# Mixture kernel on one core: convolution rotations as one 1024-column VectorE operation, and a later hand-over of the carry

## The chip, the cores and the metric

The kernel runs on one core of one Trainium2 chip. The metric is the device time of one execution in microseconds (us). Beside the plain runs there is one profiled execution; its trace carries all durations used here.

## The reference

The reference is two layers of the form `x = x + s * silu(g)`, on a normalised `x` of 2048 tokens by 512 channels. In the first layer `s` is a gated product with a per-token top-k mask, and `g` a product with ternary weights. In the second layer `g` is a 512x512 product (with low-rank experts folded in), and `s` is a small recurrent network, which the change touches. It has 2 sequences of 1024 steps, 64 channels and 4 blocks. Cut to what matters:

```python
def sconv(x, phazor_c, last_conv_c):          # x: (2, 1024, 64), per block
    p = jnp.tanh(r) * jnp.exp(1j * jnp.angle(phazor_c))
    # conv[t] = sum_{s<=t} p**(t-s) * x[s]  +  last_conv * p**(t+1), computed by FFT
    return conv.real

def body(h, p):                               # four times
    y = silu(layernorm(h, l1w, l1b))
    h = h + sconv(y, pr + 1j * pi, lr + 1j * li) * scl
    y = layernorm(h, l2w, l2b)
    y = silu(y @ w1.T + b1_) @ w2.T + b2_
    return h + y
```

## The kernel before, in words

The first 469 us of the trace are the first layer and the folding of weights; the change does not touch them. Then comes the recurrent part. Channels lie on partitions (64 for each of the two sequences, 128 in all), time steps on columns, and the 1024 steps are cut into two halves of 512 columns, `c` = 0 and 1.

The convolution is a complex recurrence with a constant factor `p = rho * e^(i*angle)`. The kernel turns the input backwards by the angle, so that the recurrence has the real factor `rho`, runs two real scans, and turns the result back. In steps, for block `l` and half `c`:

- `turn` (L1547): VectorE computes `w_re = y * rot_c`. GpSimd computes `w_im = y * rot_s` (`times_sin`, L1352).
- `scan` (L1558), twice on VectorE: `u_re` from `w_re`, then `u_im` from `w_im`. For half 0 the start value is `u0`; for half 1 it is `carry`.
- `turn_back` (L1563): VectorE computes `w_re = u_re * rot_c`, and GpSimd `w_im = u_im * rot_s` (`times_sin` again, L1352).
- `hand_over` (L1571 to L1576), half 0 only: four operations of one column on VectorE. They make `carry` from the last column of `u_re` and `u_im`, for half 1 in the next phase.
- `into_h`: VectorE adds `w_re + w_im` (L1582) and adds the scaled sum to the residual stream `h` (L1584). The latter raises `h_ready`.

The work runs in ten phases. Phase p mixes (layer norm and convolution) half `p % 2` of block `p // 2`, and feeds (layer norm and the two products of the feed-forward part) the half that phase p - 1 mixed. Order within an engine is the program's order. What matters around the change:

- TensorE (PE) begins a phase with `center_rows` (L1737), which needs the `h` that the last phase's `into_h` wrote. Then come a gate product (L1763, the 512x512 product of the second layer's `g`, cut into pieces that fill in), the variances (L1744), the spreading of the factors (L1752), the up products (L1776) and the down products (L1782). It ends with the down products. Ahead of phase 1 it does `project_in(1)` (L1730).
- VectorE: at a phase's start `variance` (`lnv`, L1529) for both halves, `widen` (L1534) and `normed` (L1542) for both, then the convolution, and last `fed` (L1589), which adds the down products to `h`. In phase 0 there is no `fed`; `h_in(1)` (L1525) and `take_means` (L1615) stand at its end. `h_in(1)` moves the projected input of half 1 from PSUM into `h`, and ACT's `squares` (L1433) of phase 1 waits for it.
- GpSimd (POOL) makes the tables `rot_c` and `rot_s` of the coming blocks, three steps of 512 columns a phase (L1335). Two steps stand at the start of a phase, behind a wait for the `h_ready` of the last `fed` (in phase 1: of phase 0's `into_h`). The two `root` operations (`lnr`, L1346) stand behind them, each of which needs `lnv`. A third table step follows behind `ln_w`, and then the two `times_sin`. From phase 7 on no table step is left, and in phase 6 one at the start.

`settled` only raises a semaphore. Every data product between engines, and between operations of one engine, goes through a counted semaphore.

Of the kernel before, what the change touches and what calls it, by code (L numbers as in the profile page):

```python
# [13 lines left out]
P = 128  # L14
# [28 lines left out]
NB = 512  # L43
# [20 lines left out]
def settled(engine, passed):  # L64


    engine.sem_inc(passed, 1)


def mixture_kernel(nc, x, wg_t, wu_t, wd_t, tern_w, ffn_bias, win_t, cols, last_cols, b1_cols,  # L70
# [7 lines left out]
    with ExitStack() as ctx:  # L78
# [43 lines left out]
        work = over_weights(4 * SEQ)  # L122
        xn = work.rearrange("p (t n) -> p t n", n=HID)
        w_re, w_im, u_re, u_im = (work[:, j * SEQ:(j + 1) * SEQ] for j in range(4))
        sq = w_re
        weff = over_weights(KH, HID)
        win = over_weights(KH, DIM)
# [150 lines left out]
        with ExitStack() as actx:  # L278
            def sb(name, shape, dt=F32):
                return actx.enter_context(nc.sbuf_tensor(name, shape, dt))  # L280
# [867 lines left out]
        with ExitStack() as bctx:  # L1148
# [20 lines left out]
            xc = sb("xc", [P, SEQ])  # L1169
            lnv = sb("lnv", [P, HALVES, 8])  # L1170
            lnr = sb("lnr", [P, HALVES, 8])
            rot_c = sb("rot_c", [P, DEPTH, NB])
            rot_s = sb("rot_s", [P, DEPTH, NB])
            tbig = sb("tbig", [P, NB])
            rho = sb("rho", [P, DEPTH])
            part = sb("part", [P, 2])
# [5 lines left out]
            def by_half(name):  # L1182
                return [sem(f"{name}{c}") for c in range(HALVES)]
# [32 lines left out]
            ln_bc = by_half("ln_bc")  # L1216
            ln_y = by_half("ln_y")
            ln_o = by_half("ln_o")
            cv_wr = by_half("cv_wr")
            cv_wi = by_half("cv_wi")  # L1220
            cv_ur = by_half("cv_ur")
            cv_ui = by_half("cv_ui")
            cv_a = by_half("cv_a")
            cv_b = by_half("cv_b")
            cv_ab = by_half("cv_ab")
            cy_t = sem("cy_t")
            cy = sem("cy")
# [25 lines left out]
            def cs(c):  # L1253
                return slice(c * NB, (c + 1) * NB)
# [55 lines left out]
            def _(pool):  # L1310
# [34 lines left out]
                    pool.wait_ge(ln_v[c], q + 1)  # L1345
                    pool.tensor_tensor(lnr[:, c, :], lnv[:, c, :], expo2[:], ALU.pow).then_inc(ln_r[c], 1)  # L1346

                def times_sin(l, c, src, ready, count, done):

                    pool.wait_ge(ready[c], count)  # L1350
                    settled(pool, pool_passed)
                    pool.tensor_tensor(w_im[:, cs(c)], src[:, cs(c)], rot_s[:, l, :], ALU.mult).then_inc(done[c], 1)  # L1352

                def residual(m):
                    if on_pool(m):
                        t = ORDERED[m]
# [26 lines left out]
                root(0, 0)  # L1383
                pool.wait_ge(ln_w[0], 1)
                tables_some(6, 8)
                times_sin(0, 0, y, ln_o, 1, cv_wi)
                times_sin(0, 0, u_im, cv_ui, 1, cv_b)
                for phase in range(1, PHASES):
                    l, c = mixing(phase)
                    k, d = feeding(phase)  # L1390
                    feeds = phase < PHASES - 1
                    if l < DEPTH:
                        if phase == 1:
                            pool.wait_ge(h_ready[0], 2)
                        else:
                            pool.wait_ge(h_ready[c], 2 * l + 1)
                        tables_some(5 + 3 * phase, 7 + 3 * phase)
                    root(2 * l, c)
                    if feeds:
                        root(2 * k + 1, d)  # L1400
                    if l < DEPTH:
                        pool.wait_ge(ln_w[d], 2 * k + 2)
                        tables_some(7 + 3 * phase, 8 + 3 * phase)
                    if l < DEPTH:
                        pool.wait_ge(tb, N_SMALL + 6 * l + 6)
                        times_sin(l, c, y, ln_o, 2 * l + 1, cv_wi)
                        times_sin(l, c, u_im, cv_ui, l + 1, cv_b)
                    elif feeds:
                        for m in range(4):
                            residual(m)  # L1410
                    else:
                        for m in range(4, TILES):
                            residual(m)

# [84 lines left out]
            def _(dve):  # L1499
# [42 lines left out]
                    dve.tensor_tensor(xc[:, cs(c)], h[:, cs(c)], bank2[c], ALU.mult).then_inc(ln_y[c], 1)  # L1542

                def turn(l, c):
                    dve.wait_ge(tb, N_SMALL + 6 * l + 6)
                    dve.wait_ge(ln_o[c], 2 * l + 1)
                    dve.tensor_tensor(w_re[:, cs(c)], y[:, cs(c)], rot_c[:, l, :], ALU.mult).then_inc(cv_wr[c], 1)  # L1547

                def scan(l, c, imaginary):
                    w, u, ready, done = (w_im, u_im, cv_wi, cv_ui) if imaginary else (w_re, u_re, cv_wr, cv_ur)  # L1550
                    dve.wait_ge(ready[c], l + 1)
                    j = int(imaginary)
                    if c == 0:
                        first = u0[:, j, l:l + 1]
                    else:
                        dve.wait_ge(cy, 2 * l + 2)
                        first = carry[:, j:j + 1]
                    dve.tensor_tensor_scan(u[:, cs(c)], rho[:, l:l + 1].to_broadcast([P, NB]), w[:, cs(c)],  # L1558
                                           first, ALU.mult, ALU.add).then_inc(done[c], 1)

                def turn_back(l, c):
                    dve.wait_ge(cv_ur[c], l + 1)
                    dve.tensor_tensor(w_re[:, cs(c)], u_re[:, cs(c)], rot_c[:, l, :], ALU.mult).then_inc(cv_a[c], 1)  # L1563

                def hand_over(l):

# [11 lines left out]

                def into_h(l, c):
                    dve.wait_ge(cv_a[c], l + 1)  # L1580
                    dve.wait_ge(cv_b[c], l + 1)
                    dve.tensor_tensor(w_re[:, cs(c)], w_re[:, cs(c)], w_im[:, cs(c)], ALU.add).then_inc(cv_ab[c], 1)  # L1582
                    dve.wait_ge(cv_ab[c], l + 1)
                    dve.scalar_tensor_tensor(out=h[:, cs(c)], in0=w_re[:, cs(c)], scalar=pcol(l, C_SCL),  # L1584
                                             in1=h[:, cs(c)], op0=ALU.mult, op1=ALU.add).then_inc(h_ready[c], 1)

                def fed(l, c):
                    dve.wait_ge(ff_2[c], l + 1)
                    dve.scalar_tensor_tensor(out=h[:, cs(c)], in0=bank1[c], scalar=bias_c[:, l:l + 1],  # L1589
                                             in1=h[:, cs(c)], op0=ALU.add, op1=ALU.add).then_inc(h_ready[c], 1)  # L1590
# [61 lines left out]
                for phase in range(PHASES):  # L1652
# [20 lines left out]
                    if l < DEPTH:  # L1673
                        turn(l, c)
                        scan(l, c, False)
                        scan(l, c, True)
                        turn_back(l, c)
                        if c == 0:
                            hand_over(l)
                        into_h(l, c)  # L1680
                        if feeds:
                            fed(k, d)
                    elif feeds:
                        output(0)
                        output(1)
                        residual(1)
                        output(2)
                        output(3)
                        fed(k, d)
                    else:  # L1690
                        residual(5)
                        residual(7)
                        for m in range(PER_HALF, TILES):
                            output(m)
                            if m > PER_HALF:
                                residual(m - 1)
                        residual(TILES - 1)
# [223 lines left out]
```

## Time and profile before

| | us |
|---|---|
| median of 3 runs | 656.93 |
| the three runs | 655.63, 656.93, 657.48 |
| the profiled execution | 658.63 |
| its span | 656.8 |
| busy in the span: PE | 614.6 |
| DVE (VectorE) | 483.6 |
| ACT | 327.6 |
| POOL (GpSimd) | 169.6 |

The span is what the rows of the trace cover; 1.83 us of the profiled execution lie outside it. A row of the timeline has the start in us, the duration in us, the engine, the line of the kernel and the operation with what it writes and reads; in brackets stands how long the engine sat idle before it and what released it. When neighbouring rows of one engine are merged, `x2` stands at the end.

### The profile page before, as it was taken

The numbers are of one execution on the slowest core, as the hardware profiler recorded it, in microseconds if no ns is written. First come the engines' busy times: TensorE is split into PE (matmuls) and PEld (weight loads), VectorE is DVE, ScalarE is ACT, GpSimd is POOL, SyncE is SP. The second block draws the span as 40 slices with busy tenths as digits, with TensorE's granted clock in tenths as the row PEclk, the third lists the DMA queues.
The fourth block names the chain that finished last, engine by engine and source line by source line (L and its number), as shares of the span: only waits on it lengthen the run. The fifth ranks groups of instructions, "written<-read, shape, count | busy, mean of one in ns | idle before, by whom it ended". The sixth has DMA issues, their size and how long they took to land. (4 is left out here: it accounts for less than half of the span.)

```text
span 656.8 us, 8597 instructions
## 1 busy us (share of the span) xinstructions
PE 614.6 (94%) x2772; PEld 448.0 (68%) x2772; DVE 483.6 (74%) x938; ACT 327.6 (50%) x547; POOL 169.6 (26%) x296
## 2 busy tenths in 40 slices
PE   4798889999999999999999999989889999999985
PEld 3687778888888888888888888846754444444432
DVE  6798887888797787778778777767777555556556
ACT  5669467447528428627725744832273333334330
POOL 1000001001001000200200100598485555543334
PEclk9988999999999999999999999989889999999997
DMA  8811000200300200110020010640020000000015
GB/s 299 316 45 65 0 1 0 97 1 0 96 0 0 96 0 0 64 32 0 0 96 0 0 65 1 227 135 1 4 63 1 0 1 0 1 0 1 0 64 193
DMA packets 17181, 32.32 MB, mean 49 GB/s; under 512 B 3224, under 2 KB 3736, under 8 KB 17152
## 3 DMA queue, kind: packets, MB, share of 16 engines
q1 hardware_dynamic: 17152, 31.97, 14.2%
q8 instruction: 14, 0.23, 0.2%
q14 instruction: 15, 0.12, 0.1%
HBM read 24.62 MB, written 7.34 MB: 49 GB/s over the span
## 5 line engine op out<-in xcount | busy, mean ns | idle before, releaser
L751 DVE TENSOR_SCALAR_CACHE_REDUCE junk_d<-k_buf,cand 128x1376 int8<-128x1376 f32 x56 | 91.9, 1640 | 0.3
L582 ACT ACTIVATE junk_a<-k_buf,cand 128x1376 int8<-128x1376 f32 x56 | 80.5, 1437 | 0.6
L563 ACT ACTIVATE s_buf<-ps_a 128x1376 f32<-128x1376 f32 x16 | 21.1, 1320 | 105.4 <-PE ps_a L988 92.6
L1015 PE MATMUL ps_a<-wd_hi,zt_hi 128*128 128x512 f32 (+1 forms) x176 | 71.8, 408 | 1.9 <-DVE zt_lo L864 1.0
L1015 PE MATMUL ps_a<-wd_hi,zt_lo 128*128 128x512 f32 (+1 forms) x176 | 69.2, 393 | 0.0
L1015 PE MATMUL ps_a<-wd_lo,zt_hi 128*128 128x512 f32 (+1 forms) x176 | 69.0, 392 | 0.0
L1763 PE MATMUL ps_b<-arena,xt 128*128 128x512 f32 x128 | 65.4, 623 | 0.0
L504 POOL TENSOR_TENSOR xres<-xres,gate 128x512 f32<-128x512 f32 x12 | 23.6, 1965 | 144.5 <-DVE gate L871 144.5
L496 POOL TENSOR_TENSOR rstd<-var_eps,expo 128x2 f32<-128x2 f32 x8 | 5.6, 705 | 204.3 <-DVE var_eps L692 204.3
L988 PE MATMUL ps_a<-wg_hi,xt_hi 128*128 128x512 f32 (+1 forms) x192 | 53.2, 386 | 1.1 <-DVE xt_lo L680 1.1
L988 PE MATMUL ps_b<-wu_hi,xt_hi 128*128 128x512 f32 (+1 forms) x192 | 51.7, 377 | 1.5 <-DVE s_buf L729 1.5
L988 PE MATMUL ps_a<-wg_hi,xt_lo 128*128 128x512 f32 (+1 forms) x192 | 51.7, 378 | 0.0
L988 PE MATMUL ps_a<-wg_lo,xt_hi 128*128 128x512 f32 (+1 forms) x192 | 51.4, 377 | 0.0
L988 PE MATMUL ps_b<-wu_hi,xt_lo 128*128 128x512 f32 (+1 forms) x192 | 50.5, 371 | 0.0
L988 PE MATMUL ps_b<-wu_lo,xt_hi 128*128 128x512 f32 (+1 forms) x192 | 49.8, 367 | 0.0
L864 DVE TENSOR_TENSOR zt_lo<-ps_t,zt_hi 128x512 fp32r<-128x512 f32 (+1 forms) x48 | 30.8, 641 | 25.3 <-ACT zt_hi L619 24.5
L1440 ACT ACTIVATE y<-xc,arena 128x512 f32<-128x512 f32 x18 | 14.7, 815 | 53.1 <-DVE xc L1542 53.1
L988 PEld LDWEIGHTS ps_a<-wg_hi,xt_hi 128*128 128x128 f32 x192 | 35.2, 195 | 7.0 <-DVE xt_lo L680 1.5
L619 ACT ACTIVATE zt_hi<-ps_t 128x512 fp32r<-128x512 f32 (+1 forms) x48 | 26.9, 563 | 25.9 <-PE ps_t L1001 21.9
L988 PEld LDWEIGHTS ps_a<-wg_lo,xt_hi 128*128 128x128 f32 x192 | 35.7, 194 | 5.8
L1015 PEld LDWEIGHTS ps_a<-wd_hi,zt_hi 128*128 128x128 f32 (+1 forms) x176 | 33.1, 188 | 9.1 <-DVE zt_lo L864 1.8
L988 PEld LDWEIGHTS ps_a<-wg_hi,xt_lo 128*128 128x128 f32 x192 | 35.3, 193 | 5.9
(229 smaller groups left out, 1285.6 us busy)
## 6 DMA issues: line engine op xcount, KB each, us to landing
xin<-in_x SPq DMA_DIRECT2D x8, 512.0 KB, 3.6
xres<-in_x SPq DMA_DIRECT2D x8, 512.0 KB, 3.4
out<-arena SPq DMA_DIRECT2D x16, 256.0 KB, 2.0
x_scratch<-xres SPq DMA_DIRECT2D x6, 512.0 KB, 3.0
arena<-x_scratch SPq DMA_DIRECT2D x3, 1024.0 KB, 11.8
m_buf<-in_wd_t SPq DMA_DIRECT2D x3, 512.0 KB, 9.8
m_buf<-in_wg_t SPq DMA_DIRECT2D x2, 688.0 KB, 5.4
k_buf<-in_wg_t SPq DMA_DIRECT2D x2, 688.0 KB, 7.9
```

The lines of the kernel that those rows point to most:

```text
L496: pool.tensor_tensor(rstd[:], var_eps[:], expo[:], ALU.pow).then_inc(ln_rs, 1)
L504: pool.tensor_tensor(row, xres[:, t, :], gate2[:, t, :], ALU.add).then_inc(x1_ready, 1)
L563: act.activation(s_buf[:, t, :], ps_a[:].rearrange("p a n -> p (a n)")[:, 0:INNER], ACT.Silu).then_inc(s_ready, 1)
L582: act.activation(junk_a[:], k_buf[:, 1, :], ACT.Sign, bias=c, scale=-1.0, accum_out=below[:, 1:2]).then_inc(act_step, 1)
L619: act.activation(zt_hi[:, c0 * P:c1 * P], ps_t[:, i % 2, 0:(c1 - c0) * P], ACT.Copy).then_inc(zt_h, 1)
L751: dve.tensor_scalar(junk_d[:], k_buf[:, 0, :], c, -float(DROP), ALU.is_lt, ALU.add, accum_out=e).then_inc(cnt_dve, 1)
L864: dve.tensor_tensor(zt_lo[:, c0 * P:c1 * P], ps_t[:, i % 2, 0:(c1 - c0) * P], zt_hi[:, c0 * P:c1 * P].bitcast(F32), ALU.subtract).then_inc ...
L988: last = pe.matmul(bank[:, c, 0:c1 - c0], xs, ws[:, k, c0:c1], start=(k == 0 and n == 0), stop=(k == KH - 1 and n == 2))
L1015: last = pe.matmul(ps_a[:, t, :], zs, ws[0:rows, c, :], start=(c == 0 and n == 0), stop=(c == CHUNKS - 1 and n == 2))
L1440: act.activation(y[:, cs(c)], xc[:, cs(c)], func, scale=w, bias=b).then_inc(ln_o[c], 1)
L1763: pe.matmul(bankg[k % 2], xt[:, n, t * P:(t + 1) * P], weff[:, n, :], start=(n == 0), stop=False)
```

## The change

GpSimd's 16 `times_sin` (two for each block and half) are gone. The two tables become one tensor `rot` with the cosine and the sine of a block side by side, and `w_re`/`w_im` and `u_re`/`u_im` are also addressed in pairs (`w_both`, `u_both`). `turn` is one VectorE operation of 2x512 columns, with `y` read twice; it raises `cv_w`, for which both scans wait. `turn_back` is one VectorE operation of 2x512 columns and waits for both scans. `hand_over` moves from between `turn_back` and `into_h` to behind `into_h` and, where there is one, behind `fed`.

```diff
+        w_both, u_both = (work[:, 2 * j * SEQ:2 * (j + 1) * SEQ].rearrange("p (j n) -> p j n", j=2) for j in range(2))
...
-            rot_c = sb("rot_c", [P, DEPTH, NB])
-            rot_s = sb("rot_s", [P, DEPTH, NB])
+            rot = sb("rot", [P, DEPTH, 2, NB])
+            rot_c, rot_s = rot[:, :, 0, :], rot[:, :, 1, :]
...
-                def times_sin(l, c, src, ready, count, done):
-
-                    pool.wait_ge(ready[c], count)
-                    settled(pool, pool_passed)
-                    pool.tensor_tensor(w_im[:, cs(c)], src[:, cs(c)], rot_s[:, l, :], ALU.mult).then_inc(done[c], 1)
...
-                times_sin(0, 0, y, ln_o, 1, cv_wi)
-                times_sin(0, 0, u_im, cv_ui, 1, cv_b)
...
-                    if l < DEPTH:
-                        pool.wait_ge(tb, N_SMALL + 6 * l + 6)
-                        times_sin(l, c, y, ln_o, 2 * l + 1, cv_wi)
-                        times_sin(l, c, u_im, cv_ui, l + 1, cv_b)
-                    elif feeds:
+                    if l == DEPTH and feeds:
...
                 def turn(l, c):
+
                     dve.wait_ge(tb, N_SMALL + 6 * l + 6)
                     dve.wait_ge(ln_o[c], 2 * l + 1)
-                    dve.tensor_tensor(w_re[:, cs(c)], y[:, cs(c)], rot_c[:, l, :], ALU.mult).then_inc(cv_wr[c], 1)
+                    dve.tensor_tensor(w_both[:, :, cs(c)],
+                                      y[:, cs(c)].rearrange("p (o n) -> p o n", o=1).to_broadcast([P, 2, NB]),
+                                      rot[:, l, :, :], ALU.mult).then_inc(cv_w[c], 1)
...
                 def turn_back(l, c):
                     dve.wait_ge(cv_ur[c], l + 1)
-                    dve.tensor_tensor(w_re[:, cs(c)], u_re[:, cs(c)], rot_c[:, l, :], ALU.mult).then_inc(cv_a[c], 1)
+                    dve.wait_ge(cv_ui[c], l + 1)
+                    dve.tensor_tensor(w_both[:, :, cs(c)], u_both[:, :, cs(c)], rot[:, l, :, :],
+                                      ALU.mult).then_inc(cv_a[c], 1)
...
                 def into_h(l, c):
                     dve.wait_ge(cv_a[c], l + 1)
-                    dve.wait_ge(cv_b[c], l + 1)
...
                         turn_back(l, c)
-                        if c == 0:
-                            hand_over(l)
                         into_h(l, c)
                         if feeds:
                             fed(k, d)
+                        if c == 0:
+                            hand_over(l)
```

## Rows read from the trace of the kernel before

**Rows 1.** Busy time by engine in one phase, PE first; then clock, DMA.

```profile
530.90:548.30 17.40, 16.94 (x62) 7.36 (x61) 9.32 (x13) 6.75 (x11) 9.35 (x7) 1.00 0.01 1
```

**Rows 2.** The chain that ended last, start of phase 3: start us, us, what.

```profile
531.04 0.76 DVE arena L1589
531.99 1.28 POOL rot_c L1335
533.44 1.06 POOL tbig L1335
534.50 1.60 POOL lnr L1346
```

**Rows 3.** Timeline, start of phase 3: VectorE's first variance.

```profile
533.74 0.17 DVE L1529 TENSOR_SCALAR lnv<-ps_b 128x8 f32<-128x8 f32 x1 [1.95 <-PE ps_b L1744]
```

**Rows 4.** Timeline, phase 3 (half 1): the convolution, and what needs it.

```profile
539.69 1.69 DVE L1547 TENSOR_TENSOR arena<-y,rot_c 128x512 f32<-128x512 f32 x1
...
541.42 2.46 DVE L1558 TENSOR_TENSOR_SCAN arena<-rho,carry,arena 128x512 f32<-128x512 f32 x2
...
545.57 2.76 PE L1782 MATMUL ps_a<-arena,w 128*64 128x512 f32 x8
...
546.06 0.69 DVE L1582 TENSOR_TENSOR arena<-arena 128x512 f32<-128x512 f32 x1 [1.60 <-POOL arena L1352]
...
546.79 0.75 DVE L1584 SCALAR_TENSOR_TENSOR arena<-arena 128x512 f32<-128x512 f32 x1
...
548.26 1.13 PE L1737 MATMUL ps_a<-arena,center 128*128 128x512 f32 x2
```

**Rows 5.** Timeline, phase 2 (half 0): turning back, hand-over, sum, next phase's first product.

```profile
526.46 0.67 DVE L1563 TENSOR_TENSOR arena<-arena,rot_c 128x512 f32<-128x512 f32 x1
526.72 1.53 POOL L1352 TENSOR_TENSOR arena<-arena,rot_s 128x512 f32<-128x512 f32 x1 [3.22 <-DVE arena L1558]
...
527.41 0.86 DVE L1574 SCALAR_TENSOR_TENSOR carry<-arena,part 128x1 f32<-128x1 f32 x1
...
528.19 0.21 DVE L1576 SCALAR_TENSOR_TENSOR carry<-arena,part 128x1 f32<-128x1 f32 x1
...
528.24 2.76 PE L1782 MATMUL ps_a<-arena,w 128*64 128x512 f32 x8
...
529.08 0.75 DVE L1584 SCALAR_TENSOR_TENSOR arena<-arena 128x512 f32<-128x512 f32 x1
...
530.93 1.13 PE L1737 MATMUL ps_a<-arena,center 128*128 128x512 f32 x2
```

**Rows 6.** Groups by line with shapes apart: VectorE's 1024-column product of two SBUF tensors.

```profile
L675 DVE TENSOR_TENSOR wd_lo<-m_buf,wd_hi 128x1024 fp32r<-128x1024 f32 x3 | 3.6, 1219 | 0.0
```

**Rows 7.** Timeline, phase 0 from its convolution on, and the start of phase 1.

```profile
489.25 0.69 DVE L1547 TENSOR_TENSOR arena<-y,rot_c 128x512 f32<-128x512 f32 x1
...
492.98 3.65 PE L1730 MATMUL ps_a<-xt,arena 128*64 128x512 f32 x16
...
495.87 0.75 DVE L1584 SCALAR_TENSOR_TENSOR arena<-arena 128x512 f32<-128x512 f32 x1
...
496.69 0.75 DVE L1525 TENSOR_SCALAR arena<-ps_a,bias_c 128x512 f32<-128x512 f32 x1
496.83 1.27 POOL L1335 TENSOR_TENSOR rot_c<-rot_c,tbig 128x512 f32<-128x512 f32 x1 [1.79 <-DVE arena L1584]
...
497.35 1.29 DVE L1615 TENSOR_TENSOR w<-w,off 128x512 f32<-128x512 f32 x1
497.47 0.63 ACT L1433 ACTIVATE arena<-arena 128x512 f32<-128x512 f32 x1 [3.79 <-DVE arena L1525]
...
498.28 1.29 POOL L1335 TENSOR_TENSOR tbig<-arena 128x512 f32<-128x512 f32 x1 [0.18 <-POOL rot_c L1335]
...
498.50 0.95 PE L1744 MATMUL ps_b<-means,arena 128*128 128x2 f32 x8
...
499.74 3.24 POOL L1346 TENSOR_TENSOR lnr<-lnv,expo 128x8 f32<-128x8 f32 x2 [0.16 <-DVE lnv L1529]
```

More of the change, by code:

```diff
@@ L1218, in mixture_kernel @@
             ln_o = by_half("ln_o")
-            cv_wr = by_half("cv_wr")
-            cv_wi = by_half("cv_wi")
+            cv_w = by_half("cv_w")
             cv_ur = by_half("cv_ur")
@@ L1223, in mixture_kernel @@
             cv_a = by_half("cv_a")
-            cv_b = by_half("cv_b")
             cv_ab = by_half("cv_ab")
@@ L1403, in _ @@
                         tables_some(7 + 3 * phase, 8 + 3 * phase)
-                    if l < DEPTH:
-                        pool.wait_ge(tb, N_SMALL + 6 * l + 6)
-                        times_sin(l, c, y, ln_o, 2 * l + 1, cv_wi)
-                        times_sin(l, c, u_im, cv_ui, l + 1, cv_b)
-                    elif feeds:
+                    if l == DEPTH and feeds:
                         for m in range(4):
                             residual(m)
-                    else:
+                    elif l == DEPTH:
                         for m in range(4, TILES):
@@ L1546, in turn @@
                     dve.wait_ge(ln_o[c], 2 * l + 1)
-                    dve.tensor_tensor(w_re[:, cs(c)], y[:, cs(c)], rot_c[:, l, :], ALU.mult).then_inc(cv_wr[c], 1)
+                    dve.tensor_tensor(w_both[:, :, cs(c)],
+                                      y[:, cs(c)].rearrange("p (o n) -> p o n", o=1).to_broadcast([P, 2, NB]),
+                                      rot[:, l, :, :], ALU.mult).then_inc(cv_w[c], 1)
                 def scan(l, c, imaginary):
-                    w, u, ready, done = (w_im, u_im, cv_wi, cv_ui) if imaginary else (w_re, u_re, cv_wr, cv_ur)
-                    dve.wait_ge(ready[c], l + 1)
+                    w, u, done = (w_im, u_im, cv_ui) if imaginary else (w_re, u_re, cv_ur)
+                    dve.wait_ge(cv_w[c], l + 1)
                     j = int(imaginary)
```

## The prediction

> **What bounds the kernel now.** I read the table of busy time by stretch first. In phase 3, taken from one `center_rows` to the next, PE is busy for 16.94 of 17.40 us, VectorE for 9.32 and GpSimd for 9.35 [rows 1]. So the recurrent part goes at PE's pace, and the two engines that the change works on have slack over a phase. The next question is whether either of them ends a wait of PE somewhere.
>
> The chain that ended last answers for the start of a phase [rows 2]. `fed` ends at 531.04 + 0.76 = 531.80. Then the chain goes through GpSimd: the table step `rot_c` at 531.99, the table step `tbig` at 533.44, and the root at 534.50. VectorE's `lnv`, for which the root waits too, was done at 533.74 + 0.17 = 533.91 [rows 3]. So the table steps, not `lnv`, let the root go in that phase, and about half a microsecond is lost there. The change keeps these table steps and their wait; it takes `times_sin` away, which stands at the end of a phase.
>
> The timeline answers for the end of a phase. In phase 3 `into_h` ends at 546.79 + 0.75 = 547.54, and the `center_rows` that needs it starts at 548.26: 0.72 us of slack [rows 4]. In phase 2 `into_h` ends at 529.08 + 0.75 = 529.83 and `center_rows` starts at 530.93: 1.10 us of slack [rows 5]. In both cases PE is in its down products until then; in phase 2 that row ends at 528.24 + 2.76 = 531.00 [rows 5]. `fed` waits for the same down products, not for the convolution. The two starts of `center_rows` are 17.33 us apart, and nothing of the convolution is in that distance.
>
> **The change part by part.**
>
> *Turning.* The product in phase 3 shows 1.69 us for 512 columns, against 0.67 for the same size in `turn_back` [rows 4, 5]; the difference is the GpSimd product beside it. A VectorE product of two 1024-column tensors in SBUF took 1.219 us where GpSimd did nothing [rows 6]. That row has another output type and no repeated operand; two separate 512-column products would be 2 x 0.67 = 1.34, which I take as the upper end. I take 1.22 for `turn` and 1.22 for `turn_back`.
>
> *Both scans.* They stay: 2.46 us for the pair [rows 4]. No GpSimd product stands beside them any more. `turn_back` now waits for the second scan too; I count 0.04 for each hand-over between dependent operations, as between 546.06 + 0.69 = 546.75 and 546.79 [rows 4].
>
> *Sum for the convolution.* From the start of `turn` to the end of `into_h`: 1.22 + 2.46 + 1.22 + 0.69 + 0.75 + 4 x 0.04 = 6.50 us. In phase 3 it was 547.54 - 539.69 = 7.85 [rows 4], so `into_h` ends 1.35 us sooner. In phase 2 the two last operations start behind the hand-over; `turn` had the same place in the phase, one period before 539.69, at 522.36, which makes 529.83 - 522.36 = 7.47 and a gain of 0.97. All of this is gained ahead of a PE that is busy with down products for another 0.72 and 1.10 us anyway. **It is worth nothing on the path**: PE reaches `center_rows` at the same time, only with more slack. The cover would have to shrink by over 2 us before this gain counted. On the other side, if both products took twice 1.22, `into_h` would end at about 547.54 - 1.35 + 2.44 = 548.63 in phase 3, 0.4 late in each phase; no row points there.
>
> *GpSimd without `times_sin`.* Sixteen products go. Behind them in GpSimd's queue stand the next phase's table steps, which wait for `fed` (released at 531.80, started at 531.99 [rows 2]), long after the old product's end at 526.72 + 1.53 = 528.25 [rows 5]. They start when they did. Worth nothing.
>
> *The moved hand-over, phases 2, 4 and 6.* Its four operations now start when `fed` ends, in the time in which VectorE waited 1.95 us for PE's variances [rows 3]. What is queued behind them is `lnv`, and for `lnv` waits the root. The trace shows what a GpSimd operation does to them. In phase 2 the first two (one tensor each) went through beside GpSimd's product, but the third, L1574, which reads two tensors in SBUF, took 0.86 us and ended at 528.27, just as GpSimd's product did at 528.25 [rows 5]. L1576 followed within 528.19 to 528.40 [rows 5]. Now GpSimd's `rot_c` starts 0.19 behind `fed`. L1574 started 527.41 - 527.13 = 0.28 behind the end of the operation ahead of the hand-over [rows 5]. So GpSimd should be first by about 0.09, L1574 ends with it at 531.99 + 1.28 = 533.27, and L1576 at about 533.4. `lnv` is due at 533.74 [rows 3]. Cost nothing, with 0.3 us in hand. Behind phase 6 GpSimd has no table step, so nothing is blocked.
>
> *The moved hand-over, phase 0.* Here there is no `fed`; `h_in(1)` stands behind it, and PE's input product ends at 492.98 + 3.65 = 496.63 [rows 7]. New end of `into_h`: 489.25 + 6.50 = 495.75, instead of 496.62 [rows 7]. `center_rows` still waits for PE's own product until 496.63, so nothing is gained. GpSimd's `rot_c` starts 0.21 behind `into_h` (496.83 against 496.62 [rows 7]), now at 495.96, and ends at 497.23. The third operation of the hand-over comes at 496.03 and is blocked until then; the fourth ends at about 497.35. So `h_in(1)` starts at about 497.35 instead of 496.69, 0.66 late. ACT's square of that half was done at 497.47 + 0.63 = 498.10 and PE's variances started at 498.50 [rows 7]: 0.40 of it is covered, less the 0.05 between ACT's end and PE. **Cost: 0.66 - 0.35 = 0.3 us**, once, since the root of phase 1 started at 499.74 directly behind `lnv` [rows 7]; the table steps will be done at about 498.5 and don't hold it.
>
> The sum is 658.63 + 0.3 = 658.9 for a profiled execution. This execution lies 1.70 us over the median of 656.93. I put the same 0.3 on the median: **657.2 us**.
>
> *A rule of the skill against the trace.* L1571 and L1572, of one column, took their 0.2 us while GpSimd's product ran, since L1574 behind them had already started at 527.41 within it [rows 5]. The Trainium skill, "SBUF — State Buffer", section "Who interferes with whom", says that `tensor_scalar` can enter a two-port mode and then contends with GpSimd, and that the first one holds the pair for its whole instruction. By the trace these two don't; if they did, the hand-over would only come a gap later, which is the second rival below.
>
> **The rivals.**
>
> *1. VectorE is first.* 0.09 us between L1574 and GpSimd's step is little. If L1574 gets in ahead, the hand-over is over at about 496.3 in phase 0, `h_in(1)` waits for PE as before, and the cost is 0; in phases 3 and 5 the first table step may start up to 0.1 later, and the root with it. Result 656.9 to 657.1. It can't be told from the forecast by the time, but by the start of `h_in(1)`.
>
> *2. The hand-over misses the gap: slower.* Between two table steps GpSimd pauses for 0.18 us [rows 7]. If L1576 doesn't get in there, it is blocked a second time until `tbig` ends. Phase 0: `tbig` would run from 497.41 for 1.06 [rows 2] to 498.47, `h_in(1)` would start at 498.55, that is 1.86 late, and the variances 1.86 - 0.35 = 1.5 late. Phases 3 and 5: `tbig` ends at 534.50, `lnv` at 534.8, and the root 0.25 behind the start of `lnv` instead of with `tbig`, at 534.9 instead of 534.50: 0.4 each. Together 2.3 us, and 659.2. Against it: L1615 began at 497.35 beside GpSimd's step (to 498.10), ended at 498.64, so it did the rest of its work directly behind 498.10, and the next step, started at 498.28, took 1.29 instead of 1.06 [rows 2, 7]. A waiting VectorE operation gets in, and GpSimd waits. But it was one operation, and here a second one must follow it; L1576 did so within 0.15 us of the release, but with no GpSimd step behind [rows 5]. It decides from the point at which L1576 starts later than 0.18 us behind GpSimd's end.
>
> *3. The convolution was on the path after all: faster.* PE's rows have modelled ends. If the down products truly ended sooner and `center_rows` waited for `into_h`, each of the eight phases could gain up to what `into_h` gains, but no more than to the next bound. Against it: phases 2 and 3 have a slack of 1.10 and 0.72 and still the same distance from the start of the down products to `center_rows`, 530.93 - 528.24 = 2.69 [rows 5] and 548.26 - 545.57 = 2.69 [rows 4]; a wait for `into_h` would make them differ. If a third of the 1.35 counted in seven phases, it would be -3.2 us: 653.8.
>
> The page "Perfetto Trace Analysis" of the Trainium skill (section "Identifying the Most-Contended Engine") says to optimise the engine with the highest occupancy first. By that rule a change that leaves PE's work alone brings nothing here; the rows above say the same for a reason of place, not of share.
>
> **How the numbers follow.** The forecast (+0.3) gets 0.50, the first rival 0.25, the second 0.12, the third 0.08, and 0.05 is for what I don't see. A measurement of this kernel can tell about 0.3% from no change, 2 us. The forecast and the first rival are within it. The second rival at +2.3 is at its edge: two thirds of it count as slower. With the unseen split evenly: faster 0.10, same 0.79, slower 0.11. The runs of before alone spread from 655.63 to 657.48, so a median can move by 1 us without a cause; the forecast with that is 656.0 to 658.3. For 8 in 10 I go from 655.5 to 659.0, which takes in most of the second rival and a small gain.
>
> **What would show it.** In the trace of after: `turn` and `turn_back` at 1.22 us each; `into_h` ending about 2 us ahead of `center_rows` in every phase, which still starts 2.7 us behind the first down product; periods of 17.3 us unchanged; L1574 at some 1.2 us behind `fed` in phases 2 and 4, and short in phase 6; `h_in(1)` 0.7 us later in phase 0, and the roots of phases 3 and 5 still behind `tbig`. The prediction is wrong if the period of the phases changes by more than 0.1 us either way, if `lnv` in phases 3 and 5 starts more than 1.95 us behind `fed`, or if a 1024-column product takes much over 1.34.

## The result, and the profile after

| | median of 13 runs, us | lowest to highest |
|---|---|---|
| before | 657.02 | 655.26 to 658.23 |
| changed | 659.28 | 657.84 to 661.35 |

The ratio is 1.0039, with a 95% interval of 1.0024 to 1.0053. The changed kernel is slower by 2.3 us by the medians (1.6 to 3.5 by the interval). A second set of 11 runs of it, beside 29 of the kernel before, gave 1.0044 (1.0030 to 1.0058). The median lies above the forecast's range, which was 657.2 within 655.5 to 659.0.

The page of the changed kernel shows PE where it was, 0.6 us more, and GpSimd with 22.4 us less:

```profile
span 657.3 us, 8564 instructions
...
PE 615.2 (94%) x2772; PEld 447.9 (68%) x2772; DVE 485.7 (74%) x938; ACT 327.3 (50%) x547; POOL 147.2 (22%) x280
```

The spans of the two profiled executions (656.8 and 657.3) can't be subtracted. The first layer, which the change does not touch, ended 2.14 us earlier in the second one: its first transposition of the recurrent part starts at 467.62, against 469.76. So I compared the traces piece by piece, from one `center_rows` to the next.

The phases from the second on are as forecast. This is phase 3 of the changed kernel, by the timeline (start us, us, engine, line, operation):

```profile
539.72 1.22 DVE L1535 TENSOR_TENSOR arena<-y,rot 128x1024 f32<-128x1024 f32 x1
...
540.98 2.46 DVE L1548 TENSOR_TENSOR_SCAN arena<-rho,carry,arena 128x512 f32<-128x512 f32 x2
...
543.54 1.23 DVE L1554 TENSOR_TENSOR arena<-arena,rot 128x1024 f32<-128x1024 f32 x1
...
544.80 0.69 DVE L1573 TENSOR_TENSOR arena<-arena 128x512 f32<-128x512 f32 x1
...
545.53 0.75 DVE L1575 SCALAR_TENSOR_TENSOR arena<-arena 128x512 f32<-128x512 f32 x1
...
545.61 2.76 PE L1773 MATMUL ps_a<-arena,w 128*64 128x512 f32 x8
...
548.29 1.13 PE L1728 MATMUL ps_a<-arena,center 128*128 128x512 f32 x2
```

They stand to [rows 4]. The products take 1.22 and 1.23 us, the convolution 546.28 - 539.72 = 6.56 us (6.50 was worked out), and `center_rows` still starts 2.68 behind the first down product, now with 2.0 us of slack. The hand-over behind phase 2 goes as worked out too:

```profile
532.03 1.26 POOL L1334 TENSOR_TENSOR rot<-rot,tbig 128x512 f32<-128x512 f32 x1 [9.72 <-DVE arena L1580]
532.11 1.21 DVE L1566 SCALAR_TENSOR_TENSOR carry<-arena,part 128x1 f32<-128x1 f32 x1
...
533.24 0.21 DVE L1568 SCALAR_TENSOR_TENSOR carry<-arena,part 128x1 f32<-128x1 f32 x1
533.48 1.06 POOL L1334 TENSOR_TENSOR tbig<-arena 128x512 f32<-128x512 f32 x1 [0.18 <-POOL rot L1334]
...
533.78 0.17 DVE L1516 TENSOR_SCALAR lnv<-ps_b 128x8 f32<-128x8 f32 x1 [0.33 <-PE ps_b L1735]
```

The third operation is blocked by GpSimd for its whole table step, the fourth gets into the gap, and `lnv` still waits for PE, for 0.33 us. It stands to [rows 2, 3] as it should.

Phase 1 is the place where most of the loss lies. From its first `center_rows` to the next it took 16.91 us before and 19.20 us (494.43 to 513.63) in the changed kernel. Its start, by the timeline, answers to [rows 7]:

```profile
493.00 0.75 DVE L1575 SCALAR_TENSOR_TENSOR arena<-arena 128x512 f32<-128x512 f32 x1
...
493.96 1.27 POOL L1334 TENSOR_TENSOR rot<-rot,tbig 128x512 f32<-128x512 f32 x1 [6.81 <-DVE arena L1575]
494.03 1.21 DVE L1566 SCALAR_TENSOR_TENSOR carry<-arena,part 128x1 f32<-128x1 f32 x1
...
494.43 1.13 PE L1728 MATMUL ps_a<-arena,center 128*128 128x512 f32 x2
...
495.16 0.21 DVE L1568 SCALAR_TENSOR_TENSOR carry<-arena,part 128x1 f32<-128x1 f32 x1
495.29 0.73 DVE L1512 TENSOR_SCALAR arena<-ps_a,bias_c 128x512 f32<-128x512 f32 x1
...
495.40 1.06 POOL L1334 TENSOR_TENSOR tbig<-arena 128x512 f32<-128x512 f32 x1 [0.18 <-POOL rot L1334]
...
496.75 1.05 PE L1735 MATMUL ps_b<-means,arena 128*128 128x2 f32 x8 [0.33 <-ACT arena L1420]
...
498.55 3.56 PE L1754 MATMUL ps_b<-arena,xt 128*128 128x512 f32 x4
```

Two things are to be seen. First, the forecast blocking: the hand-over's third operation ends with GpSimd's table step, `h_in(1)` (L1512) starts 0.86 us behind the first `center_rows`, PE runs dry for 0.33 us, and the variances start 496.75 - 494.43 = 2.32 us behind `center_rows`. Before it was 1.82. Second, something that no part of the forecast had: the gate products behind the variances take 3.56 us instead of 1.96. The busy time by stretch shows why. The columns are PE, PEld, DVE, ACT and POOL busy, then the granted clock:

```profile
494.40:498.50 4.10, 3.77 (x22) 2.43 (x20) 2.78 (x5) 1.60 (x3) 2.31 (x3) 1.00 0.02 4
498.50:502.00 3.50, 3.50 (x7) 1.33 (x7) 0.59 (x2) 0.00 (x0) 2.82 (x2) 0.54 0.00 0
```

For 3.5 us PE had a clock of 0.54, so nearly all of it at 1.2 GHz, right behind the stretch with the gap. It costs 1.6 us in the gate products and some 0.2 in the transpositions behind them.

### The profile page after: what moved, and what is told of

Same layout as the page of the kernel before. It is cut to its first block and busy times, and to the rows that moved or that the text cites. A ratio compares the mean times of both kernels' runs of the same rounds, so it can differ in the third digit from the quotient of the medians.

```text
span 657.3 us, 8564 instructions
## 1 busy us (share of the span) xinstructions
PE 615.2 (94%) x2772; PEld 447.9 (68%) x2772; DVE 485.7 (74%) x938; ACT 327.3 (50%) x547; POOL 147.2 (22%) x280
## 5 line engine op out<-in xcount | busy, mean ns | idle before, releaser
L1754 PE MATMUL ps_b<-arena,xt 128*128 128x512 f32 x128 | 67.4, 640 | 0.0
```

The source lines that it names most:

```text
L1754: pe.matmul(bankg[k % 2], xt[:, n, t * P:(t + 1) * P], weff[:, n, :], start=(n == 0), stop=False)
```

## The experiments

Two questions come first: is it the rotations or the hand-over, and is it phase 0's hand-over or the later ones? Theory 1 (T1 in the expectations) says that the late `h_in(1)` is the whole cause, through a direct delay and the low clock.

**1. The rotations alone.** On the changed kernel:

```diff
                         turn_back(l, c)
+                        if c == 0:
+                            hand_over(l)
                         into_h(l, c)
                         if feeds:
                             fed(k, d)
-                        if c == 0:
-                            hand_over(l)
```

> The changed kernel with the hand-over back in its old place ahead of the sum into h; so only the rotations are changed. Theory (T1): the whole cost lies in phase 1 and comes from the hand-over, which delays h_in(1) by some 0.85 us, lets PE run dry for 0.33 us and is followed by a stretch of PE at 1.2 GHz. Then this kernel costs nothing: 657.0 (between 656.5 and 657.5), phase 1 from its first center product to its row product 7.63 us as before, no low clock there. Rival (T2): the 1024-column rotations themselves change what PE sees (y, rot and w read and written in another rhythm). Then the cost stays: 659.3, with the low clock in phase 1.

Measured: 657.54 (12 runs) beside 657.71, ratio 1.0001 (0.9984 to 1.0018). Phase 1 took 16.91 us, at full clock. With GpSimd idle the hand-over's third operation takes 0.22 us:

```profile
494.76 0.22 DVE L1566 SCALAR_TENSOR_TENSOR carry<-arena,part 128x1 f32<-128x1 f32 x1
494.89 0.21 DVE L1568 SCALAR_TENSOR_TENSOR carry<-arena,part 128x1 f32<-128x1 f32 x1
```

The rotations alone cost nothing that these runs can tell; the interval leaves room for about 1 us either way.

**2. The hand-over alone.** On the kernel before, the same edit the other way round.

> The kernel before with nothing but the hand-over moved behind the sum into h and behind the feed-forward sum. T1: the sum into h ends at about the time of PE's center product in phase 0 (it still waits for GpSimd), the hand-over starts only then and is blocked by GpSimd's table step for 1.3 us, so h_in(1) comes over 1.5 us late. PE waits over 1 us, and the clock falls as in the changed kernel or longer: 657.0 + 1.2 + 1.7 = 660. T2 (the rotations are the cause): 657.3 at most, from the uncovered part of the delay, at full clock.

Measured: 659.88 (7 runs) beside 657.71, ratio 1.0047 (1.0030 to 1.0063). `h_in(1)` came 1.48 us behind `center_rows`, PE waited 0.95 us for it, and phase 1 took 18.13 us. The clock stayed full there in this trace, against the expectation. `center_rows` itself came 10.32 us behind the spreading product of phase 0, against 9.86 in the trace of before; experiment 5 comes back to that. The time is close to the expected 660, but in this trace by other parts: 1.22 us in phase 1, 0.3 to 0.5 ahead of it, and 0.42 in the last two phases.

**3. Only phase 0's hand-over moved on.** On the changed kernel:

```diff
-                        if c == 0:
+                        if c == 0 and phase:
                             hand_over(l)
...
                         h_in(1)
                         take_means(w2[:], KH, 2 * DEPTH, w2_s)
+                        hand_over(0)
```

> The changed kernel with the hand-over of phase 0 alone put behind h_in(1) and the subtraction of the means of w2; phases 2, 4 and 6 as changed. T1: h_in(1) on time, the cost is gone: 657.0 (656.5 to 657.5), and the hand-overs of phases 2, 4, 6 cost nothing. Rival (T3): part of the cost comes from the three later hand-overs, blocked behind fed; then 657.5 or more stays, and a later phase shows a period over 17.33 us.

Measured: 657.18 (12 runs) beside 657.71, ratio 1.0002 (0.9988 to 1.0017). Phases 1 to 7 took 16.91, 17.33, 17.32, 17.34, 17.32, 16.92 and 16.94 us, as in the kernel before. The hand-overs of phases 2, 4 and 6 cost nothing, and the whole loss sits in phase 0's.

**4. Four traces of the changed kernel.** Does the low clock come every time? These are the trace above and three more.

> The changed kernel once more, for a second trace of it. T1: the stretch of PE at 1.2 GHz in phase 1 comes again at the same place (the first gate products behind the variances of phase 1), since the delay that leads to it is fixed by the program; +2.3 us. Rival (T4): the low clock there was chance of one execution (the two traces also differ by some 2 us in the first layer); then this trace has none and the difference to before is about 0.5 us, or the runs fall in two groups.

> A third trace of the changed kernel, to see how often the low clock in phase 1 comes. So far phase 1 took 19.20 us with it in one trace and 17.97 without in the other. If it is a matter of where the earlier low stretch in phase 0 falls, the third trace shows one of these two lengths, and h_in(1) between 0.8 and 1.4 behind the first center product.

> A fourth trace of the changed kernel, for the same question. If the direct cost were all, phase 1 would be 17.4 to 18.0 in each; the mean of the runs (+2.1 us in all, 0.3 of it outside the span) asks for about 18.7 on average, so one of these two should show over 19.

Worked out from the starts of the rows of the four traces, in us:

| trace | `h_in(1)` behind `center_rows` | PE's gap ahead of the variances | variances behind `center_rows` | low clock | phase 1 |
|---|---|---|---|---|---|
| first | 0.86 | 0.33 | 2.32 | yes | 19.20 |
| second | 1.33 | 0.80 | 2.78 | no | 17.97 |
| third | 1.33 | 0.80 | 2.78 | no | 17.97 |
| fourth | 0.91 | 0.38 | 2.36 | yes | 19.26 |
| before, both traces | 0.01, -0.14 | none | 1.82 | no | 16.91 |

So it comes in two forms. With the small gap, the gap is followed by some 3.5 us of low clock. This is the fourth trace; the gate row, the last one, had taken 1.96 us in the kernel before:

```profile
496.60 1.05 PE L1735 MATMUL ps_b<-means,arena 128*128 128x2 f32 x8 [0.38 <-ACT arena L1420]
497.52 1.03 PE L1735 MATMUL ps_a<-means,arena 128*128 128x2 f32 x8
498.41 3.63 PE L1754 MATMUL ps_b<-arena,xt 128*128 128x512 f32 x4
```

and in the second trace, with the larger gap, it isn't:

```profile
497.00 1.05 PE L1735 MATMUL ps_b<-means,arena 128*128 128x2 f32 x8 [0.80 <-ACT arena L1420]
497.91 1.03 PE L1735 MATMUL ps_a<-means,arena 128*128 128x2 f32 x8
498.81 1.96 PE L1754 MATMUL ps_b<-arena,xt 128*128 128x512 f32 x4
```

The direct cost is 17.97 - 16.91 = 1.06 us in one form. In the other it is 0.5 and the clock takes another 1.8. The mean of the four is 1.7 us. Which form comes is seen half a phase earlier, at the spreading product of phase 0, where PE always has a low stretch. In the second trace it covers that product; VectorE waits longer for it, and its convolution ends later against PE:

```profile
484.56 1.11 PE L1743 MATMUL ps_a<-ident,arena 128*128 128x128 f32 x4 [2.67 <-DVE arena L1521]
485.47 1.91 PE L1754 MATMUL ps_b<-arena,xt 128*128 128x512 f32 x2
485.71 0.69 DVE L1529 TENSOR_TENSOR xc<-arena,ps_a 128x512 f32<-128x512 f32 x1 [1.21 <-PE ps_a L1743]
```

In the first trace the same product took 0.74 us and VectorE went on at 485.46 - 484.68 = 0.78 behind its start, not 1.15. The expectations of the third and fourth trace were met: the two lengths came again, one of them over 19 us. That of the second was missed. The low clock is not fixed by the program, as Theory 1 had it there, and the trace without it still costs 1.06 us in phase 1, not the 0.5 of the rival; each length comes with its own lateness.

**5. A second trace of the kernel before.**

> A second trace of the kernel before. In two kernels with its convolution the first center product came 10.3 us behind the spreading product of phase 0, against 9.86 in its own trace, because it waited for the sum into h. Expected: 9.8 to 10.3, phase 1 at 16.91, no low clock in phase 1. If it comes at 10.3, the shorter convolution of the changed kernel does gain up to 0.5 us in phase 0 in some executions, which the forecast held at nothing.

```profile
495.10 0.75 DVE L1584 SCALAR_TENSOR_TENSOR arena<-arena 128x512 f32<-128x512 f32 x1
495.77 0.74 DVE L1525 TENSOR_SCALAR arena<-ps_a,bias_c 128x512 f32<-128x512 f32 x1
...
495.91 1.13 PE L1737 MATMUL ps_a<-arena,center 128*128 128x512 f32 x2 [0.21 <-DVE arena L1584]
```

Here `center_rows` waited 0.21 us for the sum into `h`, and started 495.91 - 495.85 = 0.06 behind its end; the distance from the spreading product is 10.03 us. In the kernels of experiments 2, 6 and 7 and the second one of experiment 9, which have the old convolution, it was 10.31 to 10.33. In all that have the new one it was 9.59 to 9.75.

The wait is in the first trace of the kernel before as well. In all six traces with the old convolution `center_rows` starts 0.06 behind the end of the sum into `h`, and 3.70 to 4.31 behind the start of PE's input product. In the twelve with the new one the sum ends 0.15 to 0.76 ahead, and the distance from the input product is 3.58 or 3.59. So in phase 0 the old convolution was on the path in every trace, by 0.12 us in the first one and by up to 0.7 in others, and the shorter one gains that.

**6. The lateness alone, small.** On the kernel before, with a new semaphore `pad`:

```diff
                     if phase == 0:
+                        dve.memset(xc[:, NB:NB + 384], 0.0).then_inc(pad, 1)
+                        dve.wait_ge(pad, 1)
                         h_in(1)
```

> The kernel before with one memset of 384 columns (0.45 us) ahead of h_in(1). T1 says that 0.35 us of lateness against the end of PE's input product is covered: phase 1 between 16.9 and 17.1, no low clock, 657.0 to 657.3. If the low clock and 2 us come already here, the cost is a matter of any gap of PE and not of its length.

The memset took 0.38 us (0.45 was expected), `h_in(1)` came 0.39 behind `center_rows`, and phase 1 took 17.05 us at full clock. Time 657.15 (11 runs) beside 657.52, ratio 0.9992 (0.9981 to 1.0004). As expected: this much is covered.

**7. The lateness alone, as large as in the changed kernel.** Two such memsets.

> The kernel before, rotations and hand-over untouched, with two VectorE memsets of 384 columns of a tile that is unused at that time (some 0.45 us each) ahead of h_in(1) in phase 0. It adds only the lateness. T1: a late h_in(1) is all it takes; h_in(1) starts 0.85 to 0.9 behind PE's first center product, the variances of phase 1 come 0.5 later than before, phase 1 takes 17.4 us at full clock and up to 19.2 if the low clock follows; time 657.0 + 0.5 to + 2.3. Rival (T5): in the changed kernel it was the freer GpSimd and the shorter convolution that brought the low clock, not the gap of PE; then phase 1 takes 17.4 here and the time is 657.5.

`h_in(1)` came 0.92 behind `center_rows`, PE had a gap of 0.40, and phase 1 took 17.58 us, without low clock. The time was 659.54 (12 runs) beside 656.90, ratio 1.0039 (1.0022 to 1.0055): the same loss as that of the changed kernel, and 2 us over what the rival of a freer GpSimd gave. So the lateness alone is enough for a loss of this size. It isn't shown that the lateness alone brings the low clock, which this trace hasn't. Of the loss, phase 1 accounts for 0.67 us, the time outside the span for 0.2, and the last two phases for 0.57 (40.57 us against 40.00, by the section after the experiments).

**8. The gap filled.** On the changed kernel, one gate product of phase 1 goes ahead of the variances:

```diff
-                    fill = GATES if l < DEPTH else LAST_GATES if feeds else (0,) * len(GATES)
+                    fill = (2, 1, 1, 3, 2, 1) if phase == 1 else GATES if l < DEPTH else LAST_GATES if feeds else (0,) * len(GATES)
```

> The changed kernel, hand-over and late h_in(1) as they are, with one gate product of phase 1 moved from behind the variances to ahead of them (fill 2,1,1,3,2,1 instead of 1,2,1,3,2,1 in that phase alone). PE then has work in the 0.33 us in which it ran dry in the traces with the low clock; the variances come 0.86 later than in the kernel before, whatever h_in(1) does. If the gap of PE ahead of the variances is what the low clock of phase 1 follows, no trace shows it any more and phase 1 takes 17.8 in each; time 657.2 + 0.9 + 0.3 - 0.3 = 658.1, a good 1 us under the changed kernel. If the low clock comes from somewhere else (the place of the low stretch in phase 0), it still appears in about half of the traces, then with phase 1 at 19.5, and the time is 659.5 or more.

> The kernel with the gap filled, a second trace: phase 1 at 17.8 without low clock if the gap is the cause, 19.5 in about every second trace if not.

> The kernel with the gap filled, a third trace: as for the second, 17.8 without low clock if the gap is the cause, 19.5 in about every second trace if not.

> The kernel with the gap filled, a fourth trace: as for the second, 17.8 without low clock if the gap is the cause, 19.5 in about every second trace if not.

Phase 1 took 17.97, 17.89, 17.96 and 17.71 us in the four traces, at full clock in all. The runs gave a median of 658.85 and a mean of 658.3 (12 runs), beside a median of 657.39; the ratio is 1.0011 (0.9997 to 1.0025). This points to the gap. But only the fourth trace had `h_in(1)` early enough (0.79) to be of the form in which the low clock came; in the others it is 1.30 to 1.38, where the changed kernel had none either.

All 18 traces together say more. What tells the two forms apart is where the low stretch of phase 0 begins. These rows are of the first trace of the changed kernel and the second of the kernel before, from the start of the spreading product on (columns as above, the clock third from the end):

```profile
484.68:485.10 0.42, 0.42 (x4) 0.42 (x5) 0.00 (x0) 0.00 (x0) 0.27 (x1) 1.00 0.00 0
485.14:486.14 1.00, 1.00 (x4) 0.48 (x3) 0.68 (x2) 0.00 (x0) 0.82 (x2) 0.50 0.00 0
...
485.88:486.22 0.34, 0.34 (x3) 0.34 (x4) 0.00 (x0) 0.00 (x0) 0.19 (x1) 1.00 0.00 0
486.26:487.26 1.00, 1.00 (x4) 0.57 (x3) 0.52 (x1) 0.00 (x0) 0.84 (x1) 0.50 0.00 0
```

In both, the product starts at full clock and the low stretch begins some 0.4 us later. The first had the gap ahead of the variances of phase 1 and the low clock behind it; the second had neither. Counted over all traces:

| low stretch of phase 0 begins | gap ahead of the variances | traces | low clock in phase 1 |
|---|---|---|---|
| 0.4 to 1.1 behind the start of the spreading product | 0.33, 0.38 | 2 | both |
| the same | none | 4 (both of before, experiment 1, the fourth here) | none |
| 0.0 to 0.3 ahead of it | 0.40 to 0.95 | 4 (two changed, experiments 2 and 7) | none |
| the same | none | 8 | none |

So in these traces the low clock took both, the gap and the later place of the earlier stretch. The gap's length doesn't tell them apart: 0.38 was followed by the low clock, 0.40 in experiment 7 wasn't. Two traces with it are few, and why the place matters stays open.

**9. A better place for the table steps.** [rows 2, 3] showed the table steps holding the roots. On the kernel of experiment 3:

```diff
                         if phase == 1:
                             pool.wait_ge(h_ready[0], 2)
-                        else:
-                            pool.wait_ge(h_ready[c], 2 * l + 1)
-                        tables_some(5 + 3 * phase, 7 + 3 * phase)
+                            tables_some(8, 10)
...
                         tables_some(7 + 3 * phase, 8 + 3 * phase)
+                        pool.wait_ge(h_ready[c], 2 * l + 2)
+                        tables_some(8 + 3 * phase, 10 + 3 * phase)
```

> The kernel of the third experiment (rotations changed, phase 0's hand-over last), and in phases 2 to 6 GpSimd's two early table steps moved ahead, behind the last phase's sum into h, where GpSimd is now idle, so that they no longer hold the roots. Theory: the 0.42 us by which phases 2 to 5 are longer (17.33) than phases 1 and 6 (16.91) is the table steps ahead of the roots; now 16.91 each, 4 x 0.42 = 1.7 us less: 655.3. Rival: the steps now block VectorE's moved hand-over or the down products' sum, or another wait takes their place; then the phases stay at 17.3 and the time at 657.0.

Measured: 656.41 (12 runs) beside 656.90, ratio 0.9983 (0.9970 to 0.9996), the only kernel here that is faster than the one before by more than its interval. All seven phases took 16.90 to 16.94 us. The steps now end well ahead of `lnv`, and the root follows it directly:

```profile
511.83 1.26 POOL L1334 TENSOR_TENSOR rot<-rot,tbig 128x512 f32<-128x512 f32 x1 [6.84 <-DVE arena L1575]
513.28 1.07 POOL L1334 TENSOR_TENSOR tbig<-arena 128x512 f32<-128x512 f32 x1 [0.18 <-POOL rot L1334]
...
516.46 0.17 DVE L1516 TENSOR_SCALAR lnv<-ps_a 128x8 f32<-128x8 f32 x1 [1.95 <-PE ps_a L1736]
516.70 3.25 POOL L1345 TENSOR_TENSOR lnr<-lnv,expo 128x8 f32<-128x8 f32 x2 [2.35 <-DVE lnv L1516]
```

The same move on the kernel before, behind `times_sin` (the eighth kernel that its expectation names is the one just shown):

> The kernel before with nothing changed but the same move of GpSimd's table steps as in the eighth kernel, here behind times_sin and the sum into h. Theory: in phase 3 the sum into h ends at 547.5, the two steps take 2.5 us, and lnv comes at 551.1, so there is room here too: phases 2 to 5 at 16.91, 655.3. Rival: with times_sin on GpSimd the room is too small, the steps end behind lnv and hold the roots as before: 657.0.

Phases 16.90 to 16.92 too, so there is room for it beside `times_sin`; 656.73 (12 runs), ratio 0.9991 (0.9977 to 1.0005). In both the phases show the 1.7 us, and the runs show 1.1 and 0.6, with intervals that reach to 2.0 and 1.5. Where the rest goes isn't shown; the last two phases took 40.44 and 40.10 us in these traces, against 40.00.

**10. The time outside the span.** The mean of a run's time less its span is 1.79 to 1.83 us in all sets of the kernel before, in experiments 2 and 6 and in the second kernel of experiment 9, and 2.12 to 2.14 in all kernels with the changed rotations.

> The kernel of the third experiment with four semaphores more, which nothing uses, so that it has as many as the kernel before. The time outside the span was 1.83 us in the kernel before and in the one with the hand-over alone moved, and 2.12 to 2.14 in all with the changed rotations. If it hangs on the number of semaphores (four fewer), it goes back to 1.83. Otherwise it stays at 2.13, and something else of the program makes it.

It stayed at 2.12 (10 runs; ratio to before 1.0007, 0.9991 to 1.0022). The number of semaphores isn't it. With the two memsets of experiment 7 it was 2.00, so it moves with small edits of the program; what makes it isn't known.

## Why the prediction was wrong, point by point

**The step that failed** is the one on phase 0's hand-over, "Cost: 0.66 - 0.35 = 0.3 us, once". It had the lateness of `h_in(1)` too small and put what follows PE's gap at nothing. The traces showed 1.06 to 2.35 us in phase 1, and 0.4 to 1.1 us more in the last two phases, for which the forecast had no term. The loss goes when phase 0's hand-over stands elsewhere (experiments 1 and 3), and it comes with that hand-over alone or with an equal lateness alone (experiments 2 and 7).

*What bounds.* Right for phases 2 to 7: PE sets their period, and they stayed at 17.32 to 17.35 and 16.91 to 16.95 us.

*Turning, scans, sum.* Right: 1.22, 1.23, 2.46, and 6.56 in all against 6.50. "Worth nothing on the path" was right in phases 1 to 7 and wrong in phase 0. There the step said that `center_rows` waits for PE's own product until 496.63, which is a modelled end. It started 0.06 us behind the end of the sum, and that is the hand-over of a wait: experiment 5 finds the same 0.06 wherever the old convolution stands. So a piece of the third rival was there, worth 0.1 to 0.7 us, in a phase that it did not name.

*GpSimd without `times_sin`.* Right: nothing moved up.

*Hand-over in phases 2, 4 and 6.* Right, with the numbers: the third operation 1.21 us long behind phases 2 and 4 and 0.22 behind phase 6, the fourth in the gap, `lnv` 1.95 us behind the end of `fed` as before.

*Hand-over in phase 0.* The mechanism was right: GpSimd first, by 494.03 - 493.96 = 0.07 us (0.07 was worked out too), and `h_in(1)` behind. The size was off. The step gave a lateness of 0.66 us and a cost of 0.3; measured were 0.86 to 1.33 us, and a direct cost of 0.5 or 1.06. It had the sum into `h` end 0.93 us ahead of `center_rows`; in the four traces of the changed kernel it ended 0.2 to 0.7 ahead. 0.12 us of the difference is the wait above: without it `center_rows` comes sooner. Another 0.4 to 0.5 depends on where the low stretch of phase 0 falls, which moves the two chains against each other, and the hand-over turns this into lateness one to one. From the lateness on the step was right: less 0.35, 0.86 gives 0.5 and 1.33 gives 1.0.

*A term that was missing.* The low clock behind the gap, 1.8 us in half of the traces. The forecast counted what the gap itself takes, less the 0.35 that is covered. Nothing in it asked what a gap of PE costs beyond its length, though in the trace of before the gap of 2.67 us ahead of the spreading product of phase 0 was followed by a low stretch: the clock was 0.50 from 488 to 490 us.

*Outside the span.* 0.3 us for which the forecast had no term.

*The end.* The forecast put what lies behind phase 7 at no change. By the traces it is where the rest of the loss is, from the last `center_rows` to the end of the span. These are its starts in the kernel before and in the second trace of the changed one:

```profile
616.76 1.13 PE L1737 MATMUL ps_a<-arena,center 128*128 128x512 f32 x2
...
615.39 1.13 PE L1728 MATMUL ps_a<-arena,center 128*128 128x512 f32 x2
```

With the spans of 656.8 and 656.5 that is 40.0 and 41.1 us. The parts of the whole stretch from the spreading product of phase 0 on, in us:

| trace | to `center_rows` of phase 1 | phase 1 | phases 2 to 7 | last two phases | all |
|---|---|---|---|---|---|
| before, both traces | 9.86, 10.03 | 16.91 | 103.2 | 40.00 | 169.9, 170.1 |
| changed, first and fourth | 9.75, 9.74 | 19.20, 19.26 | 103.2 | 40.43, 40.39 | 172.6 |
| changed, second and third | 9.65 | 17.97 | 103.2 | 41.07 | 171.9 |

*The account.* By the means of these traces: 1.7 us in phase 1 and 0.7 in the last two phases, less 0.2 in phase 0, make 2.2, and 0.3 outside the span make 2.5 us. The runs say 2.3 by the medians, with an interval of 1.6 to 3.5. Over the whole stretch the two forms differ by 0.7 us, less than the 1.2 of their phase 1. That the change lengthens the last two phases isn't shown: PE has low stretches there too, and kernels that cost nothing took from 39.12 (experiment 6) to 41.46 us (experiment 1, whose trace is of one of its slowest executions). In experiment 2 it was 40.42.

*The rivals.* The first one fell: GpSimd was first each time. The second one gave 659.2, which is nearly the measured time, for a reason that did not occur: the fourth operation got into GpSimd's gap in every trace (495.16 to 495.37, ahead of `tbig` at 495.40 in the first). It had the right place in phase 0 and the right size by accident. Of the Trainium skill's rule in "SBUF — State Buffer", section "Who interferes with whom": the part that the first one keeps the shared pair for its whole instruction is what every blocked row here shows (1.21 us, against 0.22 with GpSimd idle). Its remark on `tensor_scalar` isn't put to the test by the changed kernel, whose two ran ahead of GpSimd's step (493.67 and 493.79, against 493.96). In both traces of the kernel before they took 0.20 us beside a GpSimd product, so for one column the trace shows no such contention.

## What to carry to other kernels

A cheap operation that is moved to a free place of its engine is only free if the operation behind it has slack in every execution: measure that slack over several traces, since the chains of two engines moved against each other by 0.5 us here. A start that comes just one hand-over behind another engine's end, 0.06 us here, is a wait and not a tie. Before an operation with two SBUF inputs goes behind the event that also releases GpSimd, count GpSimd's whole instruction as its length, 1.2 us here for one column. The gap that a late operation opens on PE may cost more than its length, if a low clock follows it. And a loss is to be looked for up to the end of the span, not only at the place of the edit.

## What the runs showed of the hardware

- PE at 1.2 GHz for 3.5 us behind gaps of 0.33 and 0.38 us ahead of products with 2 output columns, but not behind gaps of 0.40, 0.80 and 0.95 at the same place. In the first two the low stretch of phase 0 had begun 0.4 us behind the start of the spreading product, in the others just ahead of it.
- The low stretch of phase 0 falls differently from execution to execution: over the whole spreading product (1.11 us) or only over its end (0.74 us) or behind it (0.66 us).
- A one-column VectorE operation with two SBUF inputs took 1.20 to 1.22 us behind the start of a GpSimd product of 1.26 us, and 0.22 without it.
- The last two phases took 39.1 to 41.5 us in the traces of kernels that differ little there; PE has low stretches in all of them.
- A kernel's time outside its span differed by 0.31 us between kernels with as many input and output bytes (1.82 and 2.13), in every set of 7 or more runs, and not through four semaphores.
